# Sandwich block on eight cores: the square root, reciprocal and product of the second LayerNorm, moved from the stage of its sums to the stage of its transposes

## The reference

```python
x = x + layernorm(attention(layernorm(x)))        # 16 heads of 64, q = k = v, causal
x = x + layernorm(ffn(layernorm(x)))

def ffn(x):                                       # hidden size 4096
    h = gelu(x @ binarize(w1).T + b1)
    return h @ binarize(w2).T + b2

def layernorm(x):                                 # over the last axis
    return (x - mean(x)) / sqrt(var(x) + 1e-5)
```

## Time and profile before

| | us |
|---|---|
| runs shown | 3462.41, 3557.44 |
| their median | 3509.92 |
| the profiled execution | 3456.54 |
| its span on core 0, the slowest | 3454.9 |
| spans of the eight cores | 3445.4 to 3454.9 |
| PE busy on core 0 | 2722.1 |
| DVE, ACT, POOL busy | 1178.3, 1431.5, 360.5 |

### The profile page before, as it was taken

How to read it: one execution, slowest core, us unless ns; L and a number is a source line. 1 busy time by engine, 2 the same in 40 slices (tenths; PEclk the granted TensorE clock), 3 DMA queues, 4 the chain that set the end, 5 groups by cost and what they waited for, 6 DMA issues and landing times.

```text
span 3454.9 us, 41248 instructions; the slowest of 8 cores (3445.4 to 3454.9 us)
## 1 busy us (share of the span) xinstructions
PE 2722.1 (79%) x10596; PEld 1113.6 (32%) x10596; DVE 1178.3 (34%) x2146; ACT 1431.5 (41%) x1895; POOL 360.5 (10%) x413
## 2 busy tenths in 40 slices
PE   0288888888888888888889388888887887988886
PEld 0033333333333333333333133333333333333332
DVE  7622222212222222211111433534444444434343
ACT  1156665666557655767779011111211111112111
POOL 4410101000101010000000101010101010000100
PEclk9997877777778776778889588888889888888898
DMA  4221111111112110100000434444444354444352
GB/s 128 92 74 53 31 51 50 57 47 51 30 39 79 45 35 28 34 16 13 12 13 15 112 98 111 141 119 137 122 117 128 104 143 113 140 116 138 83 146 86
DMA packets 343394, 271.79 MB, mean 79 GB/s; under 512 B 278401, under 2 KB 278657, under 8 KB 341122
## 3 DMA queue, kind: packets, MB, share of 16 engines
q1 hardware_dynamic: 316162, 184.60, 19.3%
q0 software_dynamic: 27008, 84.57, 8.7%
HBM read 218.39 MB, written 50.59 MB: 78 GB/s over the span
## 4 chain that ended last, share of the span: by engine, by line
PE 63%; DVE 13%; issue 10%; ACT 6%; POOL 4%; DMA 3%; DVEq 0%; ACTq 0%; POOLq 0%; SPq 0%
PE ps_big L711 15%; PE ps_big L1041 12%; PE ps_big L1060 10%; PE ps_b L652 7%; PE ps_a L652 6%; PE ps_tbf L617 4%; ACT ar L719 3%; POOL ar L888 2%; ACT ar L725 2%; DMA ar<-scr_sw2t 2%; PE ps_tbf L937 2%; PE ps_tbf L504 2%; PE ps_tbf L554 2%; PE ps_a L824 2%; POOL ar L608 1%
## 5 line engine op out<-in xcount | busy, mean ns | idle before, releaser
L725 ACT ACTIVATE ar<-ps_big 128x1024 bf16<-128x1024 f32 x896 | 877.1, 1022 | 486.1 <-PE ps_big L711 475.7
L711 PE MATMUL ps_big<-ar,ar 65*128 65x512 bf16 (+3 forms) x2304 | 780.1, 419 | 46.3 <-ACT ar L725 32.0
L1041 PE MATMUL ps_big<-ar,ar 128*128 128x512 bf16 x2048 | 519.9, 419 | 78.6 <-ACT ar L1049 78.5
L1060 PE MATMUL ps_big<-ar,ar 128*128 128x512 bf16 x2048 | 453.8, 382 | 30.8 <-DVE ar L1071 19.3
L652 PE MATMUL ps_b<-ar,ar 128*65 128x512 bf16 (+3 forms) x1280 | 421.5, 415 | 16.4 <-DVE ar L731 16.1
L1049 ACT ACTIVATE ar<-ps_big,b_sb,alpha_sb 128x512 bf16<-128x512 f32 x256 | 197.1, 776 | 473.8 <-PE ps_big L1041 473.3
L652 PE MATMUL ps_a<-ar,ar 128*65 128x512 bf16 (+3 forms) x1024 | 345.0, 424 | 55.9 <-DVE ar L731 55.8
L731 DVE TENSOR_TENSOR ar<-ar,tril 128x128 bf16<-128x128 bf16 x512 | 113.7, 224 | 759.9 <-ACT ar L719 724.1
L711 PEld LDWEIGHTS ps_big<-ar,ar 65*128 65x128 bf16 x2304 | 199.1, 106 | 431.7 <-issue 391.7
L1041 PEld LDWEIGHTS ps_big<-ar,ar 128*128 128x128 bf16 x2048 | 214.1, 106 | 377.2 <-issue 185.8
L1060 PEld LDWEIGHTS ps_big<-ar,ar 128*128 128x128 bf16 x2048 | 199.5, 98 | 280.4 <-issue 44.9
(11 more groups left out here) (121 smaller groups left out, 1844.9 us busy)
## 6 DMA issues: line engine op xcount, KB each, us to landing
ar<-scr_sw1t SPq DMA_DIRECT2D x64, 1024.0 KB, 6.0
ar<-scr_sw2t SPq DMA_DIRECT2D x256, 256.0 KB, 3.1
scr_o<-ar POOLq DMA_DIRECT2D x128, 130.0 KB, 2.2
ar<-x_in SPq DMA_DIRECT2D x32, 512.0 KB, 3.3
ar<-w_in SPq DMA_DIRECT2D x32, 512.0 KB, 3.7
ar<-w_in SPq DMA_DIRECT2D x16, 1024.0 KB, 5.8
ar<-scr_o POOLq DMA_DIRECT2D x16, 1024.0 KB, 8.0
ar<-x_in POOLq DMA_DIRECT2D x8, 2048.0 KB, 15.8
```

What stands on the lines that cost most here:

```text
L711: e.matmul(psg[sp2][:, 512 * j + c0:512 * (j + 1)], bufK[hb][0:SLOT, P * kc:P * (kc + 1)], bufQ[hb][0:SLOT, 512 * w + c0:512 * (w + 1)], s ...
L725: er = s.op("act", lambda e, gp=gp, sp2=sp2: e.activation(PT[gp], psg[sp2], AF.Exp), reads=[psg_B[sp2][0], psg_B[sp2][1]], writes=[PT_B[gp]])
L1041: e.matmul(cps[pq], sw1t_sb[par][:, hc % 4, c_, :], xn2_fm[wp][:, c_, :], start=(c_ == 0), stop=(c_ == 7)),
L1060: f2=f2: e.matmul(cps[f2], g_ring[:, slot, P * t:P * (t + 1)], sw2t_sb[gb][:, k, 512 * dh:512 * (dh + 1)], start=(k == 0), stop=(k == 7)),
```

## The change

The square root, the reciprocal and the product are recorded at the start of `c_stageB1` and no longer at the end of `c_stageA2`. Nothing is computed in another way. Lines behind the place move by one in the changed kernel, and the three operations from L848, L851 and L853 to L851, L854 and L856.

```diff
@@ def c_stageA2(w):
         s.op("dve", lambda e: e.tensor_sub(varrow, e2row, tmprow),
              reads=[rows_B], writes=[rows_B])
+
+    def c_stageB1(w):
+        wp = w % 2
         s.op("act", lambda e: e.activation(tmprow, varrow, AF.Sqrt,
                                            bias=consts[0:1, 0:1]),
              reads=[rows_B, consts_B], writes=[rows_B])
...
             out=nbrow, in0=murow, scalar=-1.0, in1=arow,
             op0=ALU.mult, op1=ALU.mult),
             reads=[rows_B], writes=[rows_B])
-    def c_stageB1(w):
-        wp = w % 2
         for t in range(4):
             tp = t % 2
```

## The result

The changed kernel is slower by 0.6%: ratio 1.0063, 95% interval 1.0049 to 1.0077, which is +22 us (17 to 27) on the 3462.3 us median of ten runs of the kernel before. Its own median over eleven runs is 3532.1 us, but in six of them the cores of one or both dies had a lower granted clock, and the ratio leaves such runs out; the other five lie between 3481.5 and 3483.2 us. The profiled execution took 3487.1.

What follows compares the result with a forecast made beforehand. PE was taken as nearly always busy, waiting for Gelus ahead of group 1 and for a DVE, POOL and ACT chain in c_stageB1. +40 - 11 = +29 us on 3456.5 gave 3486 us, range 3462 to 3535.

Steps and rivals of the forecast that it cites:

- likeliest case's own range: Whole kernel: +23 to +31 us from the bounds of both places, given as 3479 to 3488 us.
- place A: After the second LayerNorm's sums, ahead of group 1: PE's wait for the first Gelu goes, gaining 11 us.
- Both bounds: Gain ahead of group 1: 9.4 us by the stretches behind c_stageA1, 13 by PE's idle time plus the last stretch's excess.
- Place B: After group 1's last matmuls, head of c_stageB1: transposes wait for the moved reciprocal and product, 5.7 us a window, 40 us.
- forecast shift of L882: In c_stageB1 on DVE: L882 starts 5.76 us later, behind the moved reciprocal and product.
- The Sqrt at place B: Behind group 1's Gelus on ACT: costs nothing, with 11.9 us of cover under the L1060 matmuls.
- L907's load: In c_stageB1 on ACT: the table load there falls away but gives nothing, since it ran while L901 was busy.
- The hidden delay: Rival, 7%: something else late at the head of c_stageB1 covers the reciprocal, leaving only the 11 us gain, 3445 us.
- The table loads on the path: Rival, 8%: ACT's removed steps were all on the path, giving 24 and 9 us; sum +7, 3464 us.
- The clock rival: Rival, 5%: PE's low clock lasts through 48 matmuls of group 2, costing 63 us more, 3549 us.

Runs made afterwards that it cites:

- e8_den: On top of e7_late_split, the softmax denominators' reciprocal (L810) moved from the head of c_stageA1 to before group 3's matmuls; ratio 0.9694 to the kernel before.
- e3_double: Changed kernel with the moved reciprocal run twice at the head of c_stageB1; ratio 1.0148 to the kernel before, +51 us.
- e1_mid: Changed kernel's Sqrt put behind group 1's Gelus, whole reciprocal and product among group 1's adds on DVE; ratio 0.9986 to the kernel before, -5 us.
- e5_late: Changed kernel with c_stageB1's four square roots moved behind group 2's Gelus and their DVE work among group 2's adds; ratio 0.9863 to the kernel before.
- e4_loads: Changed kernel with an unused constant Sqrt on ACT between group 0's and group 1's Gelus, restoring two table loads; ratio 1.0076 to the kernel before.
- e6_late_before: Kernel before, with only c_stageB1's square roots moved behind group 2's Gelus and their DVE work among group 2's adds; ratio 0.9770, -80 us.
- e7_late_split: e5_late's edits plus the moved reciprocal cut into four pieces among group 1's adds, product behind add 7; ratio 0.9762 to the kernel before, -82 us.

## Why the prediction was right or wrong, point by point

- **Direction and class.** Slower, inside 2%, was forecast with 80 and 93%, and so it came. The measured +22 us lie below the forecast +29 and just under the likeliest case's own range (+23 to +31). The change is clear of noise: the comparison can tell 0.15% here, far finer than the 2% that I took for it. The mechanism was right at both places; the size of one term was not.
- **The step that failed is the size of place A's gain.** "I take 11 us", between 9 and 13, was 15.9, and 13.6 or more on every core. Both bounds came from wrong neighbours. The stretches behind c_stageA1 (16.25 each) are not what a free stretch behind c_stageA2 takes: that is 14.5 to 16.2 us, and 106.4 to 108.0 for seven in six of the seven versions here without the wait (111.2 in e8_den). And the upper bound was built on PE's busy time and one window's excess, as if the matmuls' own time stayed at 111.8 less 1.7, or 110.1; it fell to 107.2, since in three or four windows of seven the clock is up early. The mistake in reading was to take 17.31 us, the same in five windows, for a sign that the matmuls in it were the same. It was ACT's chain that was the same. Where the clock came back early, the wait swallowed it. Why it comes back early in more windows without the wait is not shown.
- **Place B: right.** Forecast 40 us (bounds 36 and 40), measured 39.3, of which 35.8 are the later start of the transposes (7 x 5.1) and 2.9 their slower run at the low clock (granted 0.51 to 0.64 over c_stageB1, 0.66 to 0.86 before). e3_double shows the one-for-one passage that this term rested on, e1_mid that the order on DVE is its cause. For DVE's part in detail the forecast shift of L882 was 5.76 us and is 5.5, because the reciprocal starts 0.61 us after the last add's start, not 0.79.
- **The Sqrt at place B: free, right** (11.7 us of cover, 11.9 forecast). Its table load was free only as long as PE waited for DVE in group 2 anyway: where that wait was taken away (e5_late), the Gelu's reload there cost 2.5 us. **L907's load: nothing, right** (0.98 and 0.99 us).
- **The rivals.** The hidden delay is out: e3_double passed on 24.7 of 24.1 us. The table loads on the path would have taken 24 us off at place A and 9 at L907: 15.9 and nothing came, and e4_loads prices the loads at 4.9 at most. The clock rival is out: group 2's first 64 matmuls took 183.7 us in sum against 183.2 before.
- **The sum.** 3486 us was forecast for an execution like the profiled one, and that took 3487. This closeness is luck. The profiled execution is as long as its slowest core, here core 1 with 3485.5 us; core 0, from whose rows the forecast was made, took 3478.6: it grew by 23.7 us where 29 was forecast. Between the two traces six cores grew by 22 to 25 us and cores 1 and 2 by 38 and 37, and core 1's excess lies in the last window (7.7 us) and in c_stageA1 ahead of the loop (5.2), which the change does not touch. Luck too is that the median of all eleven, 3532.1, lies inside the stated range of 3462 to 3535: the number is 46 us off it, and nothing in the working led there; the range only reached so far because the two runs shown lay 95 us apart.

## What to carry to other kernels

An instruction that is moved takes its place in a queue, and costs what the queue's next customer waits for. Two instructions that take DVE 4.0 us cost 39 us in seven windows at the head of a stage that PE waits for. Whole, among adds with 1 us of idle time between them, they cost 12. They cost 1 when the long one is cut so that each piece fits into that idle time. Before moving work off one wait, look for who stands behind it at the new place on each of its engines, and there prefer the middle of a long matmul stretch to its end. And where a stretch takes the same time in window after window, look at what its length is set by before taking it for the cost of the work in it. A price borrowed from the nearest stretch of the same instructions was wrong here twice, at place A and in e6_late_before.

## What was not expected of the hardware

A wait hides what the clock does. At place A five of seven stretches of the same 64 matmuls took 17.30 or 17.31 us at granted clocks from 0.86 to 0.94, and without the wait they take 14.5 to 16.2. A second one: group 2's matmuls behind a c_stageB1 of the same instructions took 100.7 us in sum in e6_late_before and 110.6 in e7_late_split, 6 us of it by the clock alone, so that two edits worth 18 and 80 us were worth 82 together. Where the clock falls and rises again in a stage of light work decides part of what an edit is worth, and no run here shows what sets it.
